# Causal small attention: GpSimd's order of the pieces of q and k, of its clearings and of the added output bias

## The reference, cut to what matters

```python
# L1_attn_a: q, k, v, scores of a causal softmax, output projection with bias
q = apply_rope(q) * scale
k = apply_rope(k)
dots = jnp.einsum('bnih,bnjh->bnij', q, k)
dots = jnp.where(mask, jnp.float32(-100000.0), dots)
attn = jax.nn.softmax(dots, axis=-1)
o = jnp.einsum('bnij,bnjh->bnih', attn, v)
...
return o @ Wo.T + bo
# attn_block of L1_attn_b: the same shape with 4 key heads repeated, no bias at the output, residual added
```

## Time and profile before

| | us |
|---|---|
| median of three runs | 5145.84 |
| the profiled execution, its own time | 5152.51 |
| span of the profile | 5150.8 |

### The profile page before, as it was taken

One profiled execution on the slowest core, in us unless ns is written; L12 is line 12 of the kernel. 1 busy time (PEld: TensorE's weight loads), 2 busy tenths in 40 slices (PEclk: granted clock), 3 DMA queues, 4 the chain that ended last, 5 costly groups with the idle time before them and its releaser, 6 DMA issues. The chain is left out here.

```text
span 5150.8 us, 89693 instructions
## 1 busy us (share of the span) xinstructions
PE 3850.6 (75%) x25840; PEld 2732.2 (53%) x25840; DVE 3542.9 (69%) x9744; ACT 2353.8 (46%) x5537; POOL 2389.2 (46%) x3900
## 2 busy tenths in 40 slices
PE   5888797679999799458869826558775887797364
PEld 3666565556666466446656626423332665465263
DVE  5788675656666676656658757669998664687566
ACT  2444464245555466134446614345552553365142
POOL 3666442433343442446633244267775661232542
PEclk9999898789999899689989959879998999899597
DMA  5000232100000132133323211212112330232112
GB/s 224 1 0 0 94 122 84 42 27 1 1 0 1 65 121 93 37 115 104 109 79 120 92 41 40 66 48 63 63 62 71 111 117 8 82 122 73 40 41 74
DMA packets 243673, 341.37 MB, mean 66 GB/s; under 512 B 26848, under 2 KB 185968, under 8 KB 242224
## 3 DMA queue, kind: packets, MB, share of 16 engines
q1 hardware_dynamic: 230064, 309.19, 18.0%
q0 software_dynamic: 13184, 27.22, 1.5%
HBM read 182.77 MB, written 147.26 MB: 64 GB/s over the span
## 5 line engine op out<-in xcount | busy, mean ns | idle before, releaser
L522 DVE TENSOR_REDUCE l0att_rowmax<-l0att_S 128x2 f32<-128x512 f32 x512 | 339.6, 686 | 128.7 <-PE l0att_S L701 126.5
L892 POOL TENSOR_TENSOR wb_prob<-wb_prob,wb_rden 128x128 f32<-128x128 f32 (+1 forms) x512 | 248.2, 506 | 377.2 <-DVE wb_rden L1069 376.9
L1420 POOL DMA_INDIRECT results<-e_y,e_back x220 | 215.6, 980 | 418.3 <-DVE e_y L1651 399.5
L522 DVE TENSOR_REDUCE l1ffn_rowmax<-l1ffn_S 128x2 f32<-128x512 f32 x512 | 337.5, 686 | 87.6 <-PE l1ffn_S L701 83.7
L1966 POOL TENSOR_TENSOR ssm_hc<-core_AW_all,ssm_Cs 128x512 f32<-128x512 f32 x256 | 320.8, 1268 | 130.0 <-DVE core_AW_all L2112 96.9
L934 ACT ACTIVATE wb_prob<-wb_biased,wb_nmax 128x128 f32<-128x128 f32 (+1 forms) x512 | 228.6, 447 | 252.3 <-DVE wb_nmax L1062 249.4
L2211 PE MATMUL ssm_Y<-ssm_hc,core_ident 128*128 128x512 f32 x512 | 286.5, 670 | 56.7 <-POOL ssm_hc L1966 30.2
L2112 DVE TENSOR_TENSOR_SCAN core_AW_all<-core_AW_all,ssm_U 128x512 f32<-128x512 f32 x256 | 310.6, 1213 | 1.3 <-ACT core_AW_all L2055 0.4
L701 PE MATMUL l1ffn_S<-l1ffn_K,l1ffn_Q 128*128 128x512 f32 x512 | 249.5, 491 | 77.9 <-DVE l1ffn_rowmax L522 41.8
L701 PE MATMUL l0att_S<-l0att_K,l0att_Q 128*128 128x512 f32 x512 | 247.4, 487 | 63.9 <-DMA l0att_K<-bounce 48.8
L2055 ACT ACTIVATE core_AW_all<-ssm_dt,ssm_A 128x510 f32<-128x510 f32 x256 | 178.5, 716 | 221.5 <-DVE core_AW_all L2112 220.0
(11 more groups left out here) (499 smaller groups left out, 11673.7 us busy)
## 6 DMA issues: line engine op xcount, KB each, us to landing
bounce<-l0att_parts SPq DMA_DIRECT2D x128, 256.0 KB, 2.8
bounce<-l1ffn_parts SPq DMA_DIRECT2D x128, 256.0 KB, 2.8
ssm_Cs<-c_rows SPq DMA_DIRECT2D x128, 256.0 KB, 3.1
routed<-core_Y SPq DMA_DIRECT2D x8, 2048.0 KB, 23.4
l0att_Q<-bounce SPq DMA_DIRECT2D x128, 128.0 KB
l0att_K<-bounce SPq DMA_DIRECT2D x128, 128.0 KB
bounce<-l1att_parts SPq DMA_DIRECT2D x64, 256.0 KB, 2.8
l1ffn_Q<-bounce SPq DMA_DIRECT2D x128, 128.0 KB
```

The source lines that it names most:

```text
L522: dve.tensor_reduce(out=rowmax[:, jp, qt, 2 * pair:2 * pair + 2], in_=S[a % 2][:].rearrange("p (j k) -> p j k", j=2)[:, :, 0:keys(qt)], op ...
L892: ins = pool.tensor_tensor(out=prob[:, w_ % 4, a:b], in0=prob[:, w_ % 4, a:b], in1=rden[:, w_ % 4, n:n + 1].to_broadcast([P, b - a]), op=A ...
L1420: pool.indirect_dma_start(core.results, bass.IndirectOffsetOnAxis(ap=back[:, j % RING, 1:2], axis=0), y[:, j % RING, :], None).then_inc(y_ ...
```

## The change

Only the order in which GpSimd works is changed; no instruction is added or left out. `part` is cut into rotated (q, k), first_part and second_part. In the loop over rounds they stand between single clearings, clearings 12 to 14 follow at the end of their own round (where `hide(r-1, 12, 15)` stood first in the next), and where the output is added to the residual (l1att), the bias is added after clearing 3.

```diff
-            def part(n):
+            def rotated(n, x):
+
                 if rope:
-                    for x in range(2):
-                        out_of(pool, "qk"[x] * 2, n)
-                        own.step(pool.tensor_tensor(out=full[:, x, :], in0=rt[:, x, 0, :], in1=rt[:, x, 1, :],
-                                                    op=ALU.add))
+                    out_of(pool, "qk"[x] * 2, n)
+                    own.step(pool.tensor_tensor(out=full[:, x, :], in0=rt[:, x, 0, :], in1=rt[:, x, 1, :], op=ALU.add))
+
+            def first_part(n):
+                if rope:
                     own.settle()
                 else:
                     out_of(pool, "qk", n)
                 await_(pool, stored, stored.at(n - 1, 64))
                 own.step(pool.tensor_copy(parts[:, 0], full[:]))
+
+            def second_part(n):
                 own.settle()
                 pool.tensor_tensor(out=parts[:, 1], in0=full[:], in1=parts[:, 0], op=ALU.subtract)\
                     .then_inc(parted.sem, 1)
...
             for r in range(-1, SEQS + 1):
-                hide(r - 1, 12, 15)
                 if inside(r):
                     part_max(r, 1)
                 hide(r - 1, 15, 16)
                 if inside(r + 3):
                     normalise(r + 3)
-                hide(r, 0, 8)
+                hide(r, 0, 4)
+                if finish != "y_norm":
+                    last(r + 3)
+                hide(r, 4, 8)
                 if inside(r + 1):
                     part_max(r + 1, 0)
+                hide(r, 8, 10)
                 if inside(r + 3):
-                    part(r + 3)
-                hide(r, 8, 12)
-                last(r + 3)
+                    rotated(r + 3, 0)
+                hide(r, 10, 11)
+                if inside(r + 3):
+                    rotated(r + 3, 1)
+                hide(r, 11, 12)
+                if inside(r + 3):
+                    first_part(r + 3)
+                hide(r, 12, 13)
+                if inside(r + 3):
+                    second_part(r + 3)
+                if finish == "y_norm":
+                    last(r + 3)
+                hide(r, 13, 15)
                 if out_norm and inside(r - 1):
                     out_power(r - 1)
```

More of the change, by code:

```diff
@@ L412, in last, with part @@
                     advance(n)
+            def part(n):
+                for x in range(2):
+                    rotated(n, x)
+                first_part(n)
+                second_part(n)
             normalise(0)
```

## The result

The changed kernel takes 5174.93 us (median of six runs, 5164.12 to 5182.03) against 5145.96 us for the kernel before beside it (5143.51 to 5153.76): ratio 1.0053, 95% interval 1.0039 to 1.0067. By the ratio it is 27 us slower. The forecast was 5149 with 5132 to 5168 as its range, so it was too low; the rival "the DMA wait cools TensorE" had said 5171. The medians of the kernel before lay between 5141 and 5154 us in the sets of runs that follow (on one and the same chip at 5140.87 and at 5153.57), so from here on ratios are compared.

The account below looks back on a forecast made before the run. No engine bounds the whole; the clearing loop binds l1att, the store and send loop gqa. l1att -12.1, gqa +6.4, clock falls +8.7 sum to +3 us on the 5145.84 median: 5149 us, range 5132 to 5168.

Parts of the forecast that it names:

- the DMA wait cools TensorE: Rival, chance 0.16: waits at slot 8 in both causal layers lower the clock in most rounds, 22 falls, 5171 us.
- the loop through the clearings: Slot 8, k's rotation, L375, L377, clearing backlog, bias, maxima, clearing 15, weighing, slots 2 to 7; binds l1att, 20.58 us a round.
- the loop through stores and sends: Slot 8 to L377's end, then SyncE's four stores, five sends, landing, slot 8; binds gqa, 19.01 us a round.
- L377's remainder 0.5 us later: On GpSimd, clearings 11 and 12 make L377 end 0.5 us later against slot 8; bounds 0.3 and 0.8.
- The weighing's wait down to 0.6 us: In l1att, clearing 15 ends 1.6 us earlier, so TensorE's wait before weighing units 8 to 15 shrinks from 2.12 us.
- The bias at no cost in its new place: In l1att, the bias (0.73 us) after clearing 3 falls into GpSimd's 0.89 us idle time and costs nothing.
- the wait at slot 8: TensorE's new wait for K's DMA: 1.7 us in l1att, 1.8 in gqa by weight load; 1.5 to 1.6 by matmul.
- The rounds without a fall, 19.65 and 19.5 us: New round lengths of l1att and gqa with the store and send loop setting both, in place of 20.58 and 19.01.
- the landing: Store, send and landing, from L377's end to slot 8, taken as 10.8 us in both layers; bounds 10.5 and 11.1.
- a gain of 5.7: Both layers' 13 rounds together before new clock falls: l1att -12.1 us, gqa +6.4 us, sum -5.7 us.
- the last term, the falls: TensorE's clock falls after the wait at slot 8 in 6 of 26 rounds, 1.4 us each: +8.7 us (bounds 0, 36).
- The +30 us that the prediction had worked out for a fall in every round: The skill page's case: the DMA wait lowers TensorE's clock in all 26 causal-layer rounds, about +30 us.

Follow-up runs that it names:

- the pieces unbroken: The changed kernel with clearings 11 and 12 moved behind the remainder of q and k, beside 13 and 14: 5124.0 us, ratio 0.9965 to the kernel before.
- the kernel that sends first: The 5124 us kernel (clearings 11 and 12 behind the remainder), with SyncE issuing the second half's sends before the stores in both causal layers: 5242.82 us, ratio 1.018.

## Why the prediction was wrong

- That before the change l1att is bound by the loop through the clearings and gqa by the loop through stores and sends: right. The bias alone shortens l1att and leaves gqa as it was (248.6 against 247.2 us); the clearings on the other loop lengthen gqa.
- L377's remainder 0.5 us later: right (3.26 against 2.75 us). The weighing's wait down to 0.6 us: right.
- The bias at no cost in its new place: right for the clearings behind it, and alone the move is worth 25 us (0.9952). What the prediction did not see is that together with the moved pieces it costs 17 us: the loop by the clearings was no longer the one that counts, and an earlier weighing only made the wait at slot 8 longer.
- The rounds without a fall, 19.65 and 19.5 us: 0.2 us too short in l1att and 0.4 in gqa (19.8 and 19.9 measured), for the landing took 11.1 us in place of 10.8. Over 13 rounds each that is 7 to 8 us, a third of the miss: without falls the two layers would have lost 2 us, where the forecast had a gain of 5.7.
- **The step that failed** is the last term, the falls: "I take a fall in one round of four: 6 of 26", +8.7 us (6 x 1.4 is 8.4; the slip is of no weight). 14 of 26 fell, and with the one of 6.8 us they cost 24 us, 1.7 to 1.8 each; the other two thirds of the miss. The place was right, on the loop, and the price nearly. The count failed through the length of the wait at slot 8, which was put at 1.7 to 1.8 us by the weight load's account ("1.5 to 1.6" by the matmul's) and measured 2.4 (2.2). Of these 0.6 to 0.7 us the landing gives 0.3; the weighing began 2.07 us after the remainder, not 2.3, which gives 0.2; TensorE needed a little less from there to slot 8, which gives the rest. For the wait that it had, the rate was not far off: with 1.9 us of idle time, in the kernel with four idle matmuls, 7 of 26 fell, and with 1.5 none of 13. Why the landing took longer stays open.
- The rival "the DMA wait cools TensorE" had the mechanism and nearly the time, 5171, and its "from about 1.8 us of idle time on" fits the falls seen. Some luck is in the time: of its 22 falls 14 came, each a little dearer, in rounds that were longer than it had them. With the wait worked out to no better than half a microsecond and an edge inside that, its 0.16 was too little, and the range should have reached to it: its upper end at 5168 left out five of the six measured runs.
- The Trainium skill ("TensorE: Matmul & The Clock Gate", "HAM oscillation — how this bites in real kernels") describes a DMA wait in every turn that cools TensorE in every turn. The trace agrees in part: a DMA wait stood in every round of both layers, and the clock fell in seven of 13 in each. The +30 us that the prediction had worked out for a fall in every round lies near the 27 measured only because the falls were fewer and each dearer, and the rounds longer.

## What to carry to other kernels

When two loops share a piece of work, ask of every instruction that is moved on which of them it now stands: here two clearings were moved to shorten one loop and came to stand on the other, and moving them behind the remainder gave 45 us back. Ask the same again of each part of a change when another part has changed which loop counts: the bias's move gained 25 us alone and cost 17 in company. Work out the length of TensorE's longest wait in each round, and compare it with waits in the same trace after which the granted clock did and did not fall; if it lands between them, give both outcomes real chances. A wait that cannot be removed can be split in two, or filled with matmuls that nobody reads, as two runs here did.

## What the runs showed of the hardware that was not expected

In the rounds of the two causal layers, over all profiles, the granted clock fell after waits of TensorE of 1.8 us and longer by the weight load's account (the matmul's rows show 0.2 us less), and it did not fall after the eleven waits of 1.6 us (1.4 by the matmul's rows) at gqa's weighing before. Two falls are an exception, and in both a second wait began within 0.3 us of the first: 1.7 and 0.4 us in l1att with the bias put back, just behind its 13 rounds, and 1.5 and 0.9 us in gqa of the kernel with l1att alone changed. By the matmul's rows the latter are 1.28 and 0.70 us:

```profile
4051.02 0.28 PE L740 MATMUL gqa_S<-core_causal,core_ident 128*128 128x256 bf16 x1 [1.28 <-DMA gqa_K<-bounce]
...
4052.13 0.50 PE L755 MATMUL gqa_T<-gqa_Q,gqa_K 128*128 128x256 f32 x2 [0.70 <-DMA gqa_Q<-gqa_maxT]
...
4053.00:4056.00 3.00, 3.00 (x14) 2.23 (x17) 1.29 (x4) 0.89 (x3) 0.05 (x1) 0.50 0.23 78
```

After the waits of 1.9 us and longer at slot 8 of the changed kernel the clock fell in about half of the rounds, and after one of 2.3 us with the pieces unbroken it did not. So a wait of that length is not enough by itself, and what else decides was not settled here. Most low stretches lasted 3.4 us, whatever the wait before them (2.1 to 3.6 us in l1att of the changed kernel); some lasted 6.8 us, one in the changed kernel and 18 of 23 in the kernel that sends first.

Idle matmuls made a kernel faster: 280 of them by 26 us in the changed kernel (1.0053 to 1.0002), and 224 in the kernel before by 11 us (0.9978).
